# Two PSUM banks exchange tenants, and exp(k) times v moves ahead of a router part

## Time and profile before

| | |
|---|---|
| median of 3 runs | 1096.35 us (1094.07 to 1097.78) |
| profiled execution: span from first to last instruction | 1075.3 us |
| its own whole time | not listed apart; the median lies 21 us above the span |
| TensorE busy | 975.3 us, 91% of the span |
| VectorE busy | 773.2 us, 72% |
| ScalarE busy | 685.0 us, 64% |
| GpSimd busy | 632.8 us, 59% |
| mean granted TensorE clock | 0.980 of full speed |

### The profile page before, as it was taken

One profiled execution on the slowest core, in us unless ns is written; L12 is line 12 of the kernel. 1 busy time (PEld: TensorE's weight loads), 2 busy tenths in 40 slices (PEclk: granted clock), 3 DMA queues, 4 the chain that ended last, 5 costly groups with the idle time before them and its releaser, 6 DMA issues.

```text
span 1075.3 us, 21635 instructions
## 1 busy us (share of the span) xinstructions
PE 975.3 (91%) x6502; PEld 750.0 (70%) x6502; DVE 773.2 (72%) x1634; ACT 685.0 (64%) x2182; POOL 632.8 (59%) x683
## 2 busy tenths in 40 slices
PE   4668999999999999998899999989999999999996
PEld 2446667677677676776667767657788888888775
DVE  2287889889898898899988989875442222455687
ACT  0168767767767677776676776866456555566533
POOL 5664456765767567665676665312555555566654
PEclk7789999999999999999999999999999999999999
DMA  9704333353344431112211111012444544688765
GB/s 259 237 18 146 96 105 110 117 185 116 127 142 136 141 109 49 52 59 85 78 49 52 59 40 52 33 57 78 138 130 147 156 152 132 210 260 284 247 208 183
DMA packets 97872, 135.38 MB, mean 126 GB/s; under 512 B 11203, under 2 KB 83554, under 8 KB 97761
## 3 DMA queue, kind: packets, MB, share of 16 engines
q1 hardware_dynamic: 84704, 101.53, 30.7%
q0 software_dynamic: 13056, 32.47, 8.2%
HBM read 61.91 MB, written 76.23 MB: 128 GB/s over the span
## 4 chain that ended last, share of the span: by engine, by line
PE 46%; DVE 33%; issue 8%; ACT 4%; POOL 4%; DMA 2%; SPq 2%; DVEq 0%; POOLq 0%; ACTq 0%
DVE Sc L1315 7%; PE four L834 6%; PE bT L834 5%; PE four L875 5%; PE bT L589 5%; PE bM L575 4%; DVE wkv L1292 4%; DVE nmx L1317 4%; PE four L760 4%; PE bO L796 3%; PE bU L726 3%; DVE st L1230 3%; PE bM L582 2%; DMA yg<-Yt 2%; ACT Sc L1055 2%
## 5 line engine op out<-in xcount | busy, mean ns | idle before, releaser
L1055 ACT ACTIVATE Sc<-Sc,nmx 128x256 f32<-128x256 f32 x512 | 253.6, 501 | 8.2 <-DVE nmx L1317 8.2
L1063 ACT ACTIVATE PT<-bT 128x512 f32<-128x512 f32 x256 | 151.7, 592 | 136.5 <-PE bT L589 135.4
L1718 POOL DMA_INDIRECT Yt<-PT,dests x150 | 150.0, 1000 | 100.5 <-ACT PT L1134 70.0
L589 PE MATMUL bT<-idn,Sc 128*128 128x128 f32 x1024 | 161.5, 280 | 6.3 <-ACT PT L1063 5.3
L589 PEld LDWEIGHTS bT<-idn,Sc 128*128 128x128 f32 x1024 | 114.4, 141 | 71.8 <-issue 57.3
L1315 DVE TENSOR_SCALAR Sc<-four 128x1024 f32<-128x1024 f32 x128 | 155.3, 1213 | 9.5 <-PE four L760 6.1
L1317 DVE TENSOR_REDUCE nmx<-Sc 128x4 f32<-128x1024 f32 x128 | 156.2, 1220 | 4.4
L1701 POOL DMA_INDIRECT Xs<-x,slots x120 | 121.2, 1010 | 35.2 <-issue 18.3
L575 PE MATMUL bM<-mix,Wp 128*128 128x256 f32 x384 | 100.6, 408 | 35.8 <-DVE wkv L1287 20.7
L575 PEld LDWEIGHTS bM<-mix,Wp 128*128 128x128 f32 x384 | 73.5, 202 | 50.5 <-issue 38.4
L1055 ACT ACTIVATION_READ_ACCUMULATOR Sc<-Sc,nmx 128x1 f32 x512 | 99.0, 193 | 0.0
(11 more groups left out here) (220 smaller groups left out, 2024.8 us busy)
## 6 DMA issues: line engine op xcount, KB each, us to landing
Xs<-yg SPq DMA_DIRECT2D x16, 1768.0 KB, 7.9
xb<-Xs SPq DMA_DIRECT2D x152, 136.0 KB, 2.1
yg<-Yt SPq DMA_DIRECT2D x27, 512.0 KB
W<-w SPq DMA_DIRECT2D x4, 1152.0 KB, 11.2
xTs<-xT SPq DMA_DIRECT2D x16, 256.0 KB, 3.0
x<-x SPq DMA_DIRECT2D x16, 256.0 KB, 3.0
Base<-stg SPq DMA_DIRECT2D x15, 256.0 KB, 2.3
out<-acc SPq DMA_DIRECT2D x15, 256.0 KB, 4.1
```

Of the source, the lines that this page charges most:

```text
L589: last = pe.transpose(dst[:, j, t * P:(t + 1) * P], src[:, t, j * P:(j + 1) * P], idn[:, :])
L1055: last = fn(Sc[:, n % 3, m, t, :], Sc[:, n % 3, m, t, :], ACT.Exp, bias=nmx[:, n % 3, m, t:t + 1], accum_out=rs[:, s % 2, t, h:h + 1])
L1063: fn(flat(PT[:, h % RING]), bT[:, :], ACT.Copy).then_inc(a_pt.sem, 1)
L1718: pool.indirect_dma_start(Yt, bass.IndirectOffsetOnAxis(ap=dests[:, i % IDS, b:b + 1], axis=0), y_rows(i)[:, b, :], None, bounds_check=SPA ...
```

## The change

The two banks exchange tenants in slots 5 to 7. q, v, r and the positions go to `bU`; the shared expert's hidden halves and its down projection go to `bM` (`shared_bank(s)`), except for the last sequence, whose end runs in the tail and stays on `bU`. K, the context's parts and `turn_x1` stay on `bM`, the reciprocals, `Wo` and the gate on `bU`. The waits are rewritten for the new neighbours: q waits for the gate's tanh instead of `exp_k`, v no longer waits for `exp_k`, K(1) no longer waits for `copy_q(0)`, the shared expert's first half waits for `exp_k`, `rT` waits for the router's slots (`d_slots`) and `context_v` for `shared_sum` (`d_acc`), where it was the other way round; `fold_bv` waits for `tanh_r(0)`. On VectorE, `weigh_k` runs ahead of router part 1 in slot 6 instead of behind it. The number of instructions and their shapes stay the same.

```diff
+        def shared_bank(s):
+
+            return bM if s < DENSE else bU
...
                     if s == 0:
                         pe.wait_ge(s_wk, 16)
-                    elif s == 1:
-                        pe.wait_ge(a_q.sem, a_q.at(0))
                     else:
                         pe.wait_ge(a_x1T.sem, a_x1T.at(s - 1))
...
                     pe.wait_ge(g_mix.sem, g_mix.at(s, 2))
-                    pe.wait_ge(a_ek.sem, a_ek.at(s))
                     if s:
                         pe.wait_ge(a_q.sem, a_q.at(s - 1))
-                    proj(M, Wp[:, WV], mix[:, 1], ND).then_inc(p_kvr.sem, 1)
+                    proj(N, Wp[:, WV], mix[:, 1], ND).then_inc(p_kvr.sem, 1)
                 elif n == 2:
                     pe.wait_ge(g_mix.sem, g_mix.at(s, 3))
                     pe.wait_ge(d_ekv.sem, d_ekv.at(s))
-                    proj(M, Wp[:, WR], mix[:, 2], ND).then_inc(p_kvr.sem, 1)
+                    proj(N, Wp[:, WR], mix[:, 2], ND).then_inc(p_kvr.sem, 1)
 
             def context_v(s):
                 if s >= 2:
-                    pe.wait_ge(d_slots.sem, d_slots.at(s - 2))
-                if s + 1 < L:
-                    pe.wait_ge(a_thr.sem, a_thr.at(s + 1))
+                    pe.wait_ge(d_acc.sem, d_acc.at(s - 2))
+                else:
+                    pe.wait_ge(a_ek.sem, a_ek.at(s + 1))
...
             def project_q(s):
                 pe.wait_ge(a_x1T.sem, a_x1T.at(s))
-                if 0 < s < L - 1:
-                    pe.wait_ge(a_ek.sem, a_ek.at(s + 1))
-                proj(M, Wp[:, WQ], x1T, ND).then_inc(p_q.sem, 1)
+                if s == 0:
+                    pe.wait_ge(d_bo.sem, 2)
+                elif s == 1:
+                    pe.wait_ge(a_thr.sem, a_thr.at(1))
+                else:
+                    pe.wait_ge(a_gate.sem, a_gate.at(s - 2))
+                proj(N, Wp[:, WQ], x1T, ND).then_inc(p_q.sem, 1)
...
                 if n == 0:
                     if s:
-                        pe.wait_ge(d_acc.sem, d_acc.at(s - 1))
+                        pe.wait_ge(d_slots.sem, d_slots.at(s - 1))
+                    else:
+                        pe.wait_ge(a_thr.sem, a_thr.at(2))
                     pe.wait_ge(d_rr.sem, d_rr.at(s))
...
                     if c:
                         pe.wait_ge(d_sh2.sem, d_sh2.at(s, 1))
+                    elif s + 3 < L:
+                        pe.wait_ge(a_ek.sem, a_ek.at(s + 3))
+                    elif s + 2 < L:
+                        pe.wait_ge(a_x1T.sem, a_x1T.at(s + 2))
+                    elif s < DENSE:
+                        pe.wait_ge(a_v.sem, a_v.at(s + 1))
                     else:
                         pe.wait_ge(a_gate.sem, a_gate.at(s))
                     for w in range(2):
                         for j in range(ND):
-                            last = mm(N[:, w, :], W13[:, j, c, w, :], x2T[:, j, :], start=(j == 0), stop=(j == ND - 1))
+                            last = mm(cols(shared_bank(s))[:, w, :], W13[:, j, c, w, :], x2T[:, j, :], start=(j == 0), stop=(j == ND - 1))
...
             def fold_bv():
                 pe.wait_ge(s_bv, 16)
                 pe.wait_ge(s_const, 16 * 4)
+                pe.wait_ge(a_thr.sem, a_thr.at(0))
...
                 if i == FIRST + 1:
                     pe.wait_ge(a_v.sem, a_v.at(L - 1))
-                    pe.wait_ge(d_slots.sem, d_slots.at(DENSE - 1))
+                    pe.wait_ge(d_acc.sem, d_acc.at(DENSE - 1))
...
-                tt(ekv, ek, M, ALU.mult).then_inc(d_ekv.sem, 1)
+                tt(ekv, ek, cols(bU), ALU.mult).then_inc(d_ekv.sem, 1)
...
                     invert(b)
+                if B and g == 6:
+                    weigh_k(b)
                 if T and g == 6:
                     router(t, 1)
-                if B and g == 6:
-                    weigh_k(b)
```

More of the change, by code:

```diff
@@ L707, in t_chunk @@
                         pe.wait_ge(a_q.sem, a_q.at(s + 2))
[L708 to L709 removed]
+                    else:
+                        pe.wait_ge(a_gate.sem, a_gate.at(s))
                     pe.wait_ge(d_route.sem, d_route.at(s, SELECTED))
@@ L714, in t_chunk @@
                     if fresh:
-                        mm(bM[:, 0:E], ahead[:, :], picked[:, 0, :], start=True, stop=True)
-                        mm(bM[:, E:2 * E], ahead[:, :], picked[:, 1, :], start=True, stop=False)
-                        last = mm(bM[:, E:2 * E], ones[:, :], taken[:, s % 2, 1], start=False, stop=True)
-                    else:
-                        mm(bM[:, 0:2 * E], ahead[:, :], picked[:, :, :].rearrange("p t e -> p (t e)"), start=True, stop=False)
-                        last = mm(bM[:, 0:2 * E], ones[:, :], taken[:, s % 2].rearrange("p t e -> p (t e)"), start=False, stop=True)
+                        mm(bU[:, 0:E], ahead[:, :], picked[:, 0, :], start=True, stop=True)
+                        mm(bU[:, E:2 * E], ahead[:, :], picked[:, 1, :], start=True, stop=False)
+                        last = mm(bU[:, E:2 * E], ones[:, :], taken[:, s % 2, 1], start=False, stop=True)
+                    else:
+                        mm(bU[:, 0:2 * E], ahead[:, :], picked[:, :, :].rearrange("p t e -> p (t e)"), start=True, stop=False)
+                        last = mm(bU[:, 0:2 * E], ones[:, :], taken[:, s % 2].rearrange("p t e -> p (t e)"), start=False, stop=True)
                     last.then_inc(p_pos.sem, 1)
@@ L725, in t_chunk @@
                         for c in range(2):
-                            last = mm(N[:, t, :], stg[:, c, t * P:(t + 1) * P], W2[:, c, :], start=(c == 0), stop=(c == 1))
+                            last = mm(cols(shared_bank(s))[:, t, :], stg[:, c, t * P:(t + 1) * P], W2[:, c, :], start=(c == 0), stop=(c == 1))
                     last.then_inc(p_sy.sem, 1)
@@ L743, in count @@
                 if e.last + 3 < L:
-                    pe.wait_ge(a_thr.sem, a_thr.at(e.last + 3))
+                    pe.wait_ge(d_acc.sem, d_acc.at(e.last))
                 else:
@@ L1015, in tanh_r @@
                     act.wait_ge(p_q.sem, p_q.at(s - 1))
-                fn(flat(thr), M, ACT.Tanh, scale=0.5).then_inc(a_thr.sem, 1)
+                fn(flat(thr), bU[:, :], ACT.Tanh, scale=0.5).then_inc(a_thr.sem, 1)
             def copy_k(s):
@@ L1046, in copy_q @@
                     for j in range(ND):
-                        last = fn(QT[:, s % 2, m, j, :], cols(bM)[:, j, :], ACT.Identity, scale=mask[:, m:m + 1], bias=qb[:, m, j:j + 1])
+                        last = fn(QT[:, s % 2, m, j, :], cols(bU)[:, j, :], ACT.Identity, scale=mask[:, m:m + 1], bias=qb[:, m, j:j + 1])
                 last.then_inc(a_q.sem, 1)
@@ L1085, in t_chunk @@
                         act.wait_ge(s_base, 16 * s)
-                    fn(stg[:, c, :], bU[:, 0:TOK], ACT.Tanh, scale=0.5).then_inc(a_stg.sem, 1)
+                    fn(stg[:, c, :], shared_bank(s)[:, 0:TOK], ACT.Tanh, scale=0.5).then_inc(a_stg.sem, 1)
             def copy_rows(i):
```

8 lines of the change are left out of this document (4 added, 4 removed).

## The result

The median went from 1097.07 us (1094.07 to 1099.64, 4 runs) to **1122.34 us** (1121.25 to 1129.03, 4 runs), a ratio of 1.0251 with a 95% interval of 1.0208 to 1.0293. The kernel is 25 us slower. The forecast was 1102.5 with a range to 1110: right in sign, wrong in size by a factor of four.

The account below looks back on a forecast made before the run. VectorE's full queue was taken to bound the step from its middle to the down projection. Terms -0.2 + 6.3 + 1.5 - 1.9 + 0.5 + 0.1 = +6.3 us on 1096.35 gave 1102.65, said as 1102.5 us, range 1092 to 1110.

Parts of the forecast that it names:

- Part 1, the stall only moves: `weigh_k` ahead of router part 1: r's 0.86 us stall moves to the down projection; -0.2 us over twelve steps.
- The faster rival: TensorE's chain sets the body's time, so r's earlier start carries through: 1083 us, chance 0.13.
- Part 2, contention: Earlier `sum_num` on GpSimd runs beside router part 1 and holds up VectorE: +6.3 us, ends +4.8 and +12.3.
- six steps x 1.0 = 6.0: Router part 1 is 1.0 us longer in each of six steps where `sum_num` moves forward: +6.0 us.
- the six steps called unchanged: Body steps where `sum_num` stands behind a send's DMA, so earlier `weigh_k` was to change nothing there.
- the seven steps that I had named: Six steps where `sum_num` moves beside router part 1, 1.0 us each, and the last step, 0.3 us.
- Part 3, the clock: Longer TensorE pauses before the down projection halve its clock in one of six steps: +1.5 us, ends 0 and 9.
- Part 4, the banks: Bank exchange: nothing in the body; K(1) earlier at the start -1.9 us, q(15) later +0.5, tail +0.1.
- Much slower: Rival: both router operations miss the gap between GpSimd's operations, clock falls in half the steps: 1111.6 us, chance 0.13.
- r without a wait: Sign on TensorE: the r projection no longer waits for `weigh_k`.
- the new wait of the down projection: Sign on TensorE: the shared expert's down projection waits 0.6 us or more for VectorE's second hidden product.
- the steps from 225 to 398 us unchanged: Sign in the body: steps from `weigh_k` at 225 us to that at 398 us stay at 43.2 us.

Follow-up runs that it names:

- the order alone: Kernel before with only `weigh_k` moved ahead of router part 1, banks as before: 1112.05 us, ratio 1.0166; a second run 1099.53 us, ratio 1.0143.
- the banks alone: Changed kernel with `weigh_k` back behind router part 1, so only the bank exchange remains: 1092.44 us, ratio 0.9974.
- the held kernel: Changed kernel with `sum_num` on GpSimd also waiting until router part 1 is done: 1091.93 us, ratio 0.9974.
- the unused matmuls: Changed kernel with four matmuls of no use ahead of the positions, filling TensorE's pause before the down projection: 1110.55 us, ratio 1.0183.
- the held kernel's variant: The held kernel with `add_bo` moved behind `sum_den` on GpSimd: 1092.97 us, ratio 1.0009.
- the kernel before with its neighbour: Kernel before plus two GpSimd operations of `sum_num`'s shapes, result unused, running beside router part 1: 1108.91 us, ratio 1.0168.

## Why the prediction was wrong

**Part 1, the stall only moves: right.** The steps without contention are 43.18 and 43.19 us long, the down projection waits 0.86 to 0.88 us for VectorE there, and the kernel with `sum_num` held back has a body of 523.53 against 522.99 and 524.62. r's early start is worth nothing. The faster rival is out.

**Part 2, contention: the mechanism and the price of one case right, the count wrong.** This is the first step that failed, the term "six steps x 1.0 = 6.0". I took from one trace that `sum_num` stands behind the last send in the ordinary steps, and took that place as fixed. It is set by the landing of an earlier send relative to `weigh_k`. Moving `weigh_k` 2.6 us forward alone would have put `sum_num` 3.6 to 4.6 us behind it, while router part 1 is over 3.3 us behind it. In the order alone that left five of those six steps untouched. The new banks let the send land up to 1.6 us sooner in four of the six steps called unchanged, and `sum_num` came 2.5 to 3.5 us behind `weigh_k`, inside the router part. Both halves of the change are needed for that, and I had priced the banks at nothing there. In two of the four steps the conversion L1391 and the comparison L1397 were caught and cost 2.5 us together, in the two others L1402 alone cost 1.4 and 1.0. The price was also too low in three of the steps that I had named: their `sum_num` came 1.5 to 1.9 us behind `weigh_k`, again behind a DMA, and router part 1 took 4.5 us and not 3.7. The sum is +16.3 us instead of +6.3, beyond the upper end of +12.3 that I had worked out for six steps; 9.1 us of it fell in the seven steps that I had named and 7.2 in the four others. The pattern does not come from contended steps that feed themselves: the same short waits stand in the banks alone and in the held kernel, where there is no contention.

**Part 3, the clock: the price of a short fall right, the count wrong.** A fall of 3.4 us costs 1.5 to 1.6 us here as there (3.56 or 3.47 against 1.97); one of 6.8 us costs 1.8 on the down projection (3.78) and slows what follows it. I allowed one fall, and six (9 us) as the extreme; there were nine stretches in the body, three of them of double length. The second failed step. The pause ahead of the down projection was 1.6 to 2.9 us in 11 steps, as each us of contention is a us of pause. The matmuls that fill it won 10.9 us of body. Of the 30.9 us of the body, its twelve router parts are 14.5 us, and the other 16.4 us are what the clock cost, as far as the experiments tell the two apart.

**Part 4, the banks: right within the noise at both ends, but not in the body.** K(1) began at 46.13 us in the changed kernel and ended at 48.60 (forecast 48.15 to 49.9, was 50.17). q(15) did have to wait for the gate, 0.43 us (forecast 0.5):

```profile
723.92 1.97 PE L579 MATMUL bU<-wkv,Wp 128*128 128x256 f32 x8 [0.43 <-ACT gth L1094]
```

The banks alone gave 0.9974, -2.8 us (-5.1 to -0.7 by its interval), where the sum of part 4 was -1.3 (of -1.9, +0.5 and +0.1). What the part left out is that the banks move the landing of the sends; by themselves that costs nothing.

**The rivals.** "Much slower" named 1111.6 us and was nearest, by luck. Its mechanism, the missed gap, is not what happened in the steps it spoke of: where `sum_num` began 0.8 us behind `weigh_k`, L1383 always passed in 0.19 us. Of the signs that I had listed, r without a wait and the new wait of the down projection came; the one that failed first was "the steps from 225 to 398 us unchanged".

**The 21 us between span and median** I had put down to what lies around the span. They were an execution quicker than most. It did not enter the sum.

**What stays open.** Why the new banks let some of the sends land sooner. That they do is shown by four profiles (the banks alone, the changed kernel twice, the held kernel); with the unused matmuls the short waits fall in partly other steps, and what happens to the DMA itself is open. That the rest of the loss goes through the start of `sum_num` is shown by fixing that start, which leaves no cost of the banks. Also open is which pause lets the clock fall. In the 14 profiles no down projection with a pause of up to 1.05 us ran slower than 2.00 us. Above that the pause alone does not decide: in the held kernel 1.47 and 1.93 us were not followed by a fall and in its variant 1.17 was (2.54 us); in the changed kernel 1.60 and one of 1.90 were, another 1.90 and two of 2.58 were not. Four falls in the bodies met no down projection at all (at 535.4 us in the changed kernel, at 381.0 and 514.2 in the held kernel's variant, at 521.3 in the kernel before with its neighbour).

## What to carry to other kernels

Before an operation is moved ahead of others on one engine, ask what its result releases on other engines, whether that can hold them up (here GpSimd's tensor operations did), and at what time it runs in each step. A place behind a DMA in one trace is not a fixed place: price the case in which it comes loose for every step, not only for those in which it is loose now. A change that is free by itself can still move what another one stands on: the banks alone cost nothing and the order alone 1.7%, and together they cost 2.5%. A stall that "only moves" to TensorE is not free once something adds to it, because the clock can fall in the longer pause; here 14.5 us of small operations in the body cost about as much again.

## What the runs showed of the hardware

A TENSOR_SCALAR, CAST or TENSOR_TENSOR of VectorE on SBUF that starts while GpSimd is inside a tensor operation of 1.04 to 1.3 us ends 0.02 to 0.06 us after it: L1380 took 1.02 us and not 0.17. L1397, the largest of them, took 1.37 and not 0.28 and ended 0.15 us after it. The Trainium skill (GPSIMD Engine Reference, Key points) names this contention for VectorE instructions in a 2-port mode or with two SBUF inputs. L1397 has two SBUF inputs, and the trace agrees; L1380 has one, and no run here shows its mode. L1383, which starts in the gap of 0.08 us, takes its 0.19 us.

The later part of an indirect DMA's time on GpSimd can hold such an operation too. In the step at 181 us L1380 started at 182.15 and ended with the DMA, at 182.50 against 181.54 + 0.99 = 182.53. If a tensor operation follows the DMA at once, the VectorE operation stands through both: L1391 started at 183.55, 0.27 us before `sum_num`, and would have been done in 0.16. The second longest case in the changed kernel (the longest is L1380's 1.77 us at 690.28), VectorE and then GpSimd:

```profile
503.26 1.69 DVE L1383 TENSOR_TENSOR msk<-sc,grank 128x32 f32<-128x32 f32 x1
```

```profile
502.86 0.97 POOL L1715 DMA_INDIRECT Xs<-x,slots  x1 [0.31 <-issue]
503.84 1.06 POOL L1681 TENSOR_TENSOR wkv<-wkv,eu 128x512 f32<-128x512 f32 x1
```

It started 0.58 us before `sum_num`, of its own length 0.19, and ended 0.05 us after `sum_num`'s first operation. In router part 1 of the 14 profiles, where a tensor operation followed the DMA within 0.1 us, 20 of 21 operations of these three kinds that started 0.3 us or more into the DMA took longer than their own time, and none of 28 that started earlier. Where none followed, 48 of 56 TENSOR_SCALARs and CASTs that started 0.5 to 0.8 us into it did, but only 3 of 31 TENSOR_TENSORs.

The maxima (0.25 us) and the reductions (0.16, 0.18 and 0.37) of the same part kept their times within 0.01 us in all 14 profiles, whatever GpSimd did beside them.
